# Second-layer attention keys: head tiles kept zero by construction and filled by transfers, instead of masked copies on GpSimd

## The reference, cut to what matters

```python
# w_qkv: (8, 16, 48), one block a group of 16 channels; 16 heads of 8 channels
qkv = grouped_linear(x, w_qkv, None).reshape(B, N, 3, H, D)
qkv = jnp.transpose(qkv, (2, 0, 3, 1, 4))
q, k, v = (qkv[0] * scale, qkv[1], qkv[2])
attn = jax.nn.softmax(jnp.einsum('bhnd,bhmd->bhnm', q, k), axis=-1)
out = jnp.einsum('bhnm,bhmd->bhnd', attn, v)
```

## Time and profile before

| | us |
|---|---|
| median of 3 runs (lowest, highest) | 984.76 (979.02, 986.0) |
| the profiled execution's own time | 984.84 |
| its span, first to last instruction | 983.1 |
| busy in the span: TensorE, VectorE, ScalarE, POOL | 792.4, 649.1, 524.2, 344.6 |

### The profile page before, as it was taken

The page is one execution under the profiler, slowest core; times in us unless marked ns, Lnnn a source line. Parts: engine busy times, 40 slices in busy tenths (PEclk is TensorE's granted clock), DMA queues, the critical chain, the costliest instruction groups (busy, mean ns, idle before and its releaser), DMA issues. The chain is left out here.

```text
span 983.1 us, 12967 instructions
## 1 busy us (share of the span) xinstructions
PE 792.4 (81%) x4212; PEld 497.0 (51%) x4212; DVE 649.1 (66%) x1290; ACT 524.2 (53%) x970; POOL 344.6 (35%) x389
## 2 busy tenths in 40 slices
PE   3547888988898889999989899789989888527850
PEld 2233444555454667787767544345344444227740
DVE  3135568676663777776768696488898876347853
ACT  1013454545556677776757456456656656217740
POOL 3413775543532000000005345653453542133425
PEclk9987999999999999999999979899999999659985
DMA  4251331102110490000002112210110200011013
GB/s 125 48 95 21 85 81 35 34 22 46 30 24 2 137 285 6 1 1 1 1 8 57 43 42 63 60 35 17 38 25 18 58 4 10 4 54 56 32 34 84
DMA packets 56414, 44.75 MB, mean 46 GB/s; under 512 B 6598, under 2 KB 47387, under 8 KB 56347
## 3 DMA queue, kind: packets, MB, share of 16 engines
q1 hardware_dynamic: 55323, 41.82, 16.8%
q0 software_dynamic: 1024, 2.10, 0.7%
HBM read 14.67 MB, written 14.55 MB: 30 GB/s over the span
## 5 line engine op out<-in xcount | busy, mean ns | idle before, releaser
L926 ACT ACTIVATE ring<-single 128x512 f32<-128x512 f32 (+3 forms) x512 | 253.1, 517 | 226.3 <-PE single L1176 218.8
L1554 DVE TENSOR_REDUCE mneg<-pair 128x2 f32<-128x1024 f32 (+3 forms) x256 | 258.5, 1022 | 87.7 <-PE pair L1160 33.2
L1176 PE MATMUL single<-q_op,k_op 104*128 104x512 f32 (+3 forms) x512 | 216.5, 443 | 17.8 <-ACT ring L926 9.2
L1156 PE MATMUL pair<-k_op,q_op 96*128 96x512 f32 (+3 forms) x512 | 172.1, 415 | 42.2 <-DVE mneg L1554 22.6
L786 POOL TENSOR_SCALAR k_op<-k_stk,cst 104x512 fp32r<-104x512 f32 x64 | 100.0, 1577 | 276.2 <-DMA k_stk<-hl 258.5
L1176 PEld LDWEIGHTS single<-q_op,k_op 122*128 122x128 f32 (+1 forms) x512 | 97.9, 197 | 98.6 <-ACT ring L926 72.6
L1156 PEld LDWEIGHTS pair<-k_op,q_op 120*128 120x128 f32 (+1 forms) x512 | 98.9, 207 | 86.8 <-DVE mneg L1554 44.8
L1192 PE MATMUL p_o<-ring,vaug 128*9 128x512 f32 (+3 forms) x1024 | 116.1, 526 | 1.0 <-ACT ring L926 0.9
L721 POOL TENSOR_SCALAR_AFFINE_SELECT ring<-ring 128x256 f32<-128x256 f32 x128 | 52.3, 408 | 149.4 <-ACT ring L926 149.2
L955 ACT ACTIVATE ring<-pair,cols 128x512 f32<-128x512 f32 x136 | 86.1, 685 | 33.8 <-PE pair L1236 27.5
L1600 DVE TENSOR_TENSOR ring<-ring,single 128x1024 f32<-128x1024 f32 x60 | 73.3, 1221 | 45.5 <-ACT ring L955 44.4
(11 more groups left out here) (294 smaller groups left out, 1306.4 us busy)
## 6 DMA issues: line engine op xcount, KB each, us to landing
xs<-zero SPq DMA_DIRECT2D x10, 1024.0 KB, 10.1
q_op<-hl SPq DMA_DIRECT2D x96, 64.0 KB, 2.0
stage<-in_L_ffn_W_dram SPq DMA_DIRECT2D x8, 512.0 KB, 4.5
stage<-in_L_ffn_rW_dram SPq DMA_DIRECT2D x6, 512.0 KB, 5.1
k_op<-hl SPq DMA_DIRECT2D x48, 64.0 KB
k_stk<-hl SPq DMA_DIRECT2D x48, 64.0 KB, 2.0
xb<-xs SPq DMA_DIRECT2D x15, 128.0 KB, 2.0
xs<-yb SPq DMA_DIRECT2D x15, 128.0 KB, 1.7
```

Of the source, the lines that this page charges most:

```text
L926: exp_done.by(act.activation(ring[:, n % 8, lo:T], singles[n % 2][:, lo:T], ACT.Exp), (L, n))
L1156: ins = pe.matmul(both[:, i, 0:hi], r32(qs[:, P * qt:P * (qt + 1)]), r32(ks[:, 0:hi]), start=i == 0 or L == 1 or qt >= 2, stop=L == 1)
L1176: st_full.by(pe.matmul(singles[n % 2][:, lo:T], r32(ks[:, P * kc:P * (kc + 1)]), r32(qs[:, lo:T]), start=True, stop=True), (L, n))
L1554: s_taken.by(dve.tensor_reduce(mneg[:, G % 2, 2 * p:2 * p + 2, qt], both[:, :, 0:hi], axis=AX.X, op=ALU.max, negate=True), (L, m))
```

## The change

All of it is in the second layer.

- The weights of q and k are no longer permuted by head; a head's 8 channels are 8 neighbouring rows.
- A new tile `hl1` of eight slots replaces `hl`: queries high, high, low, zero; keys high, low, high, ones in two of eight rows. ScalarE writes the high part twice in one instruction (its input broadcast, 1024 output columns instead of 512).
- The query operand is filled by one transfer of a group (32 rows of four slots become 128 rows). The keys of a head are filled by one transfer (8 rows of four slots become 32 rows of the head's own tile of 128). These tiles, `k_op1[0]` to `k_op1[2]`, four heads each, are zeroed once by POOL and never written outside the head's 32 rows. So a group has five transfers (256 rows of 2 KB) where there were six (192 rows).
- `mask` and `k_masked` are gone; the first max unit of a group waits on the transfers. All matmuls of scores read 128 rows instead of 96 or 104.
- The key tiles have three buffers instead of four: the keys of group G are moved once the last exponential of group G-3 is done. Tiles 1 and 2 lie on memory of the dense stage and are zeroed when it ends.
- SP's order is rewritten: `m_dma(G)`, then `head1_dma(G + 2)`. The pieces of expert weights are loaded and split two a row instead of all eight in row 4.

```diff
-        k_op1 = put("k_op1", [P, 4 * GH, T], at=at_op)
+        hl1 = put("hl1", [P, 8, T], at=at_op + 16 * KB)
         q_op1 = put("q_op1", [P, NG, T], at=at_op + 32 * KB)
-        k_stk = put("k_stk", [P, NG, T], at=at_op + 40 * KB)
+        k_op1 = [put(f"k_op1{i}", [P, GH, T], at=at_op + at * KB) for i, at in enumerate((40, 0, 8))]
...
+        HIGH1, LOW1 = {"q": slice(0, 2), "k": slice(4, 7, 2)}, {"q": 2, "k": 5}
...
             def head1_dma(G):
                 r, g = G // NG, G % NG
...
+                taken.wait_ge(sp, ("q", NB + r))
+                if G >= NG:
+                    exp_done.wait_ge(sp, (1, GH * NT * (G - NG + 1) - 1))
+                sp.dma_start(q_op1[:, g, :], hl1[32 * g:32 * g + 32, 0:4, :]).then_inc(head_rows1[g], 16)
+                taken.wait_ge(sp, ("k", NB + r))
+                if G >= 3:
+                    exp_done.wait_ge(sp, (1, GH * NT * (G - 2) - 1))
+                elif G:
+                    sp.wait_ge(k_zero, G)
+                    apart(sp)
+                for j in range(GH):
+                    sp.dma_start(k_op1[G % 3][32 * j:32 * j + 32, j, :],
+                                 hl1[32 * g + HD * j:32 * g + HD * (j + 1), 4:8, :]).then_inc(head_rows1[g], 16)
...
-            for g in range(NG):
-                head1_dma(g)
+            for G in range(3):
+                head1_dma(G)
             expert1(0)
             expert1(1)
             m_dma(1, 0)
...
+            for G in range(1, 4 * NG):
+                m_dma(1, G)
+                if G + 2 < 4 * NG:
+                    head1_dma(G + 2)
+                if G % NG == 0 and G // NG < NB:
+                    expert1(G // 2)
+                    expert1(G // 2 + 1)
...
-                pool.tensor_scalar(by_dim(w_q[1][:, :]), by_head(w_qkv[:, 0:D]), SCALE1, None, ALU.mult)
-                pool.tensor_copy(by_dim(w_k1[:, :]), by_head(w_qkv[:, D:2 * D]))
+                pool.tensor_scalar(w_q[1][:, :], w_qkv[:, 0:D], SCALE1, None, ALU.mult)
+                pool.tensor_copy(w_k1[:, :], w_qkv[:, D:2 * D])
...
-            pool.memset(k_stk[96:P, :, :], 1.0).then_inc(k_ones, 1)
+            steps.step(pool.memset(hl1[:, 3, :], 0.0))
+            steps.step(pool.memset(k_op1[0][:, :, :], 0.0))
+            pool.tensor_scalar(hl1[:, 7, :], hl1[:, 3, :], cst[:, C_HM:C_HM + 1], None, ALU.add).then_inc(k_ones, 1)
             pool.wait_ge(k_ones, 1)
+            y_step.wait_ge(pool, units[-1])
+            for i in (1, 2):
+                pool.memset(k_op1[i][:, :, :], 0.0).then_inc(k_zero, 1)
...
             for s in range(NB, STAGES):
                 add_bias(s)
-                mask(G + 3)
...
+                weights1(2 * (s - NB))
+                if s > NB:
                     modulate(s - 1)
...
+                weights1(2 * (s - NB) + 1)
+                if s > NB:
                     scatter(s - 1)
...
-                        k_masked.wait_ge(pe, G)
+                        pe.wait_ge(head_rows1[G % NG], H_ROWS1 * (G // NG + 1))
```

More of the change, by code:

```diff
@@ L40 @@
 NBLK = T * NB // 256 + E1 - 1
-C_N = C_HM + GH
+C_N = C_HM + 1
 B_MS, B_TRI, B_ONE = 0, P, 2 * P
@@ L75, in constants @@
     c[:, C_IOTA:C_IOTA + 16] = np.arange(16)
-    for j in range(GH):
-        c[:, C_HM + j] = ((p < 96) & (p % GH == j)) | (p == 96 + j) | (p == 96 + GH + j)
+    c[:, C_HM] = p % HD < 2
     b = c[:, C_N:]
@@ L402, in build @@
         head_rows1 = [sem(f"head_rows1_{g}") for g in range(NG)]
-        k_masked = sig("k_masked", list(range(4 * NG)))
         rope_rows = sem("rope_rows")
@@ L407, in build @@
         gathered = [sem(f"gathered{r}") for r in range(NB)]
-        k_ones = sem("k_ones")
+        k_ones, k_zero = sem("k_ones"), sem("k_zero")
         block = ctx.enter_context(nc.Block())
@@ L438, in build @@
         acc = [p_o, p_m, p_o, p_m]
-        M_ROWS, H_ROWS, R_ROWS = 32, 16 * 6, 16 * 6
+        M_ROWS, H_ROWS, H_ROWS1, R_ROWS = 32, 16 * 6, 16 * 5, 16 * 6
         TERM = [(0, 0, 1), (0, 1, 0)]
+        HIGH1, LOW1 = {"q": slice(0, 2), "k": slice(4, 7, 2)}, {"q": 2, "k": 5}
         def by_head(ap):
@@ L524, in head1_dma @@
                 r, g = G // NG, G % NG
-                if G >= NG:
-                    exp_done.wait_ge(sp, (1, 16 * (G - NG) + 15))
-                elif G == 0:
+                if G == 0:
                     sp.wait_ge(k_ones, 1)
                     apart(sp)
[L530 to L534, removed]
+                taken.wait_ge(sp, ("q", NB + r))
[11 more added lines that the diff above has]
+                                 hl1[32 * g + HD * j:32 * g + HD * (j + 1), 4:8, :]).then_inc(head_rows1[g], 16)
             def m_dma(L, G):
@@ L541, in m_dma @@
                     else:
-                        dst = q_op1[96 + GH * part:96 + GH * (part + 1), G % NG, :]
+                        dst = q_op1[3 + 4 * part:P:32, G % NG, :]
                     sp.dma_start(dst, mT[:, part, :]).then_inc(m_rows, 16)
@@ L775, in scatter @@
                                             xn3[:, t, :], None).then_inc(scattered, 16)
[L777 to L791, removed]
             for s in range(NB, STAGES):
-                G = NG * (s - NB)
                 add_bias(s)
-                mask(G + 3)
[L796 to L799, removed]
-                    modulate(s - 1)
[L801 to L811, removed]
+                weights1(2 * (s - NB))
+                if s > NB:
+                    modulate(s - 1)
+                weights1(2 * (s - NB) + 1)
+                if s > NB:
                     scatter(s - 1)
-                if s < STAGES - 1:
-                    mask(G + 6)
             modulate(STAGES - 1)
@@ L866, in part @@
                         for g in range(NG):
-                            act.wait_ge(head_rows1[g], H_ROWS * (s - NB))
+                            act.wait_ge(head_rows1[g], H_ROWS1 * (s - NB))
                     elif s:
@@ L872, in part @@
                     w = ("q", "k").index(name)
-                    hi_ready.by(act.activation(r32(hl[:, 2 * w, :]), src[:, :], ACT.Copy), key)
+                    if L:
+                        hi_ready.by(act.activation(r32(hl1[:, HIGH1[name], :]), src[:, :].unsqueeze(1).broadcast_to([P, 2, T]), ACT.Copy), key)
+                    else:
+                        hi_ready.by(act.activation(r32(hl[:, 2 * w, :]), src[:, :], ACT.Copy), key)
                 elif name == "rs":
@@ L1133, in operands @@
                     return q_op0[0:96 + K, n, :], k_op0[0:96 + K, n, :]
-                rows_in = 96 if K == 24 else 104
-                return q_op1[0:rows_in, G % NG, :], k_op1[0:rows_in, GH * ((G + 2) % 4) + j, :]
+                return q_op1[:, G % NG, :], k_op1[G % 3][:, j, :]
             def max_unit(L, m):
@@ L1479, in part @@
                     n = 2 * (name == "k")
-                    take(key, dve.tensor_tensor(r32(hl[:, n + 1, :]), src[:, :], hl[:, n, :], ALU.subtract))
+                    hi, lo = (hl1[:, 2 * n, :], hl1[:, LOW1[name], :]) if L else (hl[:, n, :], hl[:, n + 1, :])
+                    take(key, dve.tensor_tensor(r32(lo), src[:, :], hi, ALU.subtract))
                 elif name[:2] == "mt":
```

## The result

The changed kernel takes 967.39 us (median of 4 runs, 965.12 to 970.95), the kernel before 984.68 us (4 runs); the ratio is 0.9836, 95% interval 0.981 to 0.9862. Faster by 1.6%, against a forecast of 969.0 us. The profiled execution has a span of 965.1 us where the one before had 983.1.

A forecast was written before the change was run, and what follows sets the result against it. TensorE, the busiest engine, was taken to stand still for POOL's late masks. Waits 12.7 + clock 5.2 + VectorE 2.0 - double copy 3.7 - weight pieces 0.4 = 15.8 us, from 984.8 to 969.0 us; range 958 to 983.

The forecast's parts named there:

- The waits removed: Second layer: all five waits of max units for POOL's masks go, a gain of 12.7 us.
- The clock: Three half-clock stretches behind mask waits run at full clock: gain 5.2 us, bounds 3.5 to 6.1.
- three signs of being wrong: Max units waiting for key transfers, freed time as TensorE waits for VectorE in rows 5 and 6, clock falling in new places.
- VectorE beside POOL: Norm ends and small VectorE operations in the second layer run faster without masks: gain 2.0 us, bounds 0 to 6.
- Double copy: ScalarE writes high parts of q and k twice: 0.46 us more, eight times, 3.7 us lost, bounds 0 to 5.
- Weight pieces: Six of eight move from row 4 to rows 5 to 7 and may hold VectorE: 0.4 us lost, bounds 0 to 14.
- third rival: Each of six POOL weight subtractions of 2.35 us holds a VectorE operation on the path: 14 us back, 983; chance 0.07.
- Transfers: Keys in three buffers: 7.6 us from gate to first max unit, 3.9 needed, slack 3.7 us, so no cost.
- second rival: Keys come too late with three buffers, 12 groups wait; at 8.6 us landing 1004 us; chance 0.05.
- 128-row matmuls, zeroing, lead: Wider score matmuls cost nothing, zeroing key tiles nothing (bounds 0 to 1 us), and the lead stays as long as before.
- first rival: VectorE's reductions are just as late in rows 5 and 6, so only 8.4 us gained, 976.4 us; chance 0.15.

The follow-up runs named there:

- before_two_a_row: The kernel before, masks kept, with only the weight pieces changed: two loaded and split in each row; 985.99 us, ratio 1.0017.
- before_keys_earlier: The kernel before, masks kept, with query and key transfers issued one group earlier and row 4's masks ahead of its last four weight pieces; 973.17 us, ratio 0.9877.
- idle_masks_row4: The changed kernel with all weight pieces in row 4 and 64 POOL multiplications that nobody waits for put back; 973.47 us, ratio 0.9892.

## Why the prediction was right, and where it was not

**The time**: 969.0 forecast, 967.39 measured. Rows 4 to 7 give 9.0 + 2.8 + 0.2 + 3.8 = 15.8 us, by luck exactly the forecast sum; another 1.9 us lies before the layer's first exponential, 1.5 of it already at 307 us, where the kernels do the same work, and counts for nothing. The sum hides errors that cancel: with the pieces in row 4 the rows would have given 21.9 us where the forecast, without its term for the pieces, had 16.2, and the pieces took 6.1 of them back where it had 0.4.

**The waits removed**: right in size (12.7 us gone, no wait for POOL left). Wrong in cause: "they start late ... behind two pieces of weights". POOL had done those pieces and stood idle for 7.24 us before the masks. What the masks waited for was SyncE's order, which the change also rewrote: `before_two_a_row` takes pieces and their loads away and leaves 2.44 of the 6.13 us, and in `before_keys_earlier`, with the transfers issued earlier, no max unit waits for POOL. Removing the masks was one way to win those 6.2 us of lead; issuing the transfers earlier was another, worth 12 of the 15 to 17 us.

**The clock**: half right. The three stretches at half clock of the earlier trace rows are gone; a new one of 3.3 us came (711.8), 1.7 us back by the reckoning of the forecast. "The granted clock falls in new places" and freed time as waits of TensorE for VectorE in rows 5 and 6 were two of the three signs of being wrong that the prediction named, and both are in the new profile. They came from the pieces. (The lower bound of 3.5 us for this term does not follow from what is said beside it: half of the two stretches' 4.35 and the 0.9 of the third are 3.1.)

**VectorE beside POOL**: 2.0 us forecast; 2.2 us for 40 masks in rows 5 to 7 of `idle_masks_row4`, from one execution of each kernel, which can differ by 1.4 us in a row. It agrees in size and is not a proof.

**Double copy**: 3.7 us forecast, mis-sized. About 0.2 us a row is measured in the quads; the two kernels' times differ by 1.7 us within overlapping intervals. I counted each copy whole; of its 0.43 us an idle gap of ScalarE two exponentials later takes back 0.36, and the gap in the dense stage takes all.

**Weight pieces**: 0.4 us forecast; 8.5 us measured (970.12 against 961.63). This is the term that failed. The mechanism was written down as the third rival with the right row, but with a chance of 0.07 and "six operations" as its worst; two holds of 2.2 us did it, since a hold starves `p_m` and TensorE, and behind one of them the clock falls. I had put the price at the operation held and not at the chain behind it. (Its own sum was off too: six times 0.1 is 0.6.) In the rows of single executions the term is 6.1 to 7.5 us; the interval on the medians' 8.5 is some 3 us to either side.

**Transfers**: nothing, as forecast, but with 1.6 to 1.9 us to spare and not 3.7. The second rival (late keys) was half as far away as I said. Two steps of that working failed. The gate was read one exponential early: group 1's last one ends at 605.39, not at 604.41, which left 7.0 us and not 7.6 (603.53 to 610.49 in the changed kernel). And the chain of issues and landing takes 5.24 us, not 3.9. The gate also holds 13 groups, not 12.

**128-row matmuls, zeroing, lead**: nothing, as forecast. The shortest matmul of 128 rows is 387 ns, of 96 rows 388.

**The first rival** (VectorE takes POOL's place) did not happen: with the pieces in row 4, rows 5 and 6 fall to 64.3 and 64.4 us. The gain is then 9.1 + 5.0 + 4.0 + 3.8 = 21.9 us, with the double copy already paid, 2 more than the 19.9 that the forecast's gains add up to.

**Open**: why quad 18 of `before_keys_earlier` is still 7.7 us long was not tried apart; it holds masks, `add_bias` and late pieces at once, three of VectorE's operations on four elements take 0.6 to 1.1 us in its neighbourhood, and TensorE waits 1.2 and 0.9 us for VectorE. Nor is it shown why the clock fell behind one wait of 2.6 us and not behind the other.

## What to carry to other kernels

When a stage waits for an engine, look one link further back in that engine's own idle time before blaming its work: POOL's masks were waited for while POOL itself waited 7 us for a transfer, and a changed order of issues alone won 12 us where taking the work away won 15 to 17, or 23 with the weight pieces left in row 4. When work is moved to even out an engine, ask which short operations of the neighbour it will now stand beside, and price the chain behind the held operation. If it can't be moved, cut it: four instructions of a quarter did as well as moving it.

## What the runs showed of the hardware

- A POOL subtraction of 128x1024 held VectorE operations on four elements, with both inputs in SBUF, for 2.2 us (0.16 alone); in four instructions of 128x256 for 0.60 and 0.66 us. The four took 2.78 us on POOL instead of 2.37. An operation with one tensor input (`TENSOR_SCALAR`, 128x4) was held for 2.23 us as well.
- A ScalarE copy from PSUM with its input read twice took 1.025 us for 1024 output columns, 0.597 for 512.
- Four transfers of 8 rows of four slots into 32 rows of 2 KB took SyncE 2.89 us, three of 32 rows to 32 rows 1.80 to 1.83.
- A wait of TensorE of 2.62 us (710.88) was followed by 3.3 us at half clock, as waits of 6.1, 1.8 and 2.5 us had been by 5.3, 3.5 and 3.4 us in the kernel before. One of 2.60 us (644.34), and one of 2.0 us in the kernel before (721.13), were not.
